# The last stage of an audio tower on one Trainium2 core: query and key parts stored so that each row of the stack is one run of memory

## What is computed

```python
def _L1_ffn_ref(x, hl_w, hl_b, wq, wk, wv, gate_w, ...):   # x: 32 x 375 x 64, nh=4 heads, ne=4 experts, d=16
    sx = jnp.einsum('bsh,ndh->bnsd', x, hl_w) + hl_b[None, :, None, :]
    q = jnp.einsum('bnsd,neod->bneso', sx, wq)
    k = jnp.einsum('bnsd,nod->bnso', sx, wk)
    v = jnp.einsum('bnsd,nod->bnso', sx, wv)
    scores = jnp.einsum('bnesd,bntd->bnest', q, k) * d ** 0.5 + causal
    att = jax.nn.softmax(scores, axis=-1)
    qkv = jnp.einsum('bnest,bntd->bnesd', att, v)
    ...
```

## Time and profile before

| what | us |
|---|---|
| median of 3 timed runs | 3450.6 (3449.06 to 3461.65) |
| the profiled execution | 3409.64 |
| its span, first to last instruction | 3407.9 |
| PE busy in it | 3063.6 (90%) |
| DVE, ACT, POOL busy | 2626.5, 1815.3, 1298.5 |

### The profile page before, as it was taken

The page is one execution under the profiler, slowest core; times in us unless marked ns, Lnnn a source line. Parts: engine busy times, 40 slices in busy tenths (PEclk is TensorE's granted clock), DMA queues, the critical chain, the costliest instruction groups (busy, mean ns, idle before and its releaser), DMA issues. The chain is left out here.

```text
span 3407.9 us, 81191 instructions
## 1 busy us (share of the span) xinstructions
PE 3063.6 (90%) x24976; PEld 2182.4 (64%) x24976; DVE 2626.5 (77%) x7757; ACT 1815.3 (53%) x4488; POOL 1298.5 (38%) x1365
## 2 busy tenths in 40 slices
PE   0799999999999799998999974999999999999995
PEld 0588888888788644445777752666666666666663
DVE  4788888888888578875888854688778778877883
ACT  0255555555555455554766631466556555555652
POOL 1443444434344144440000003355455445444532
PEclk9899999999999899996888865899999999989995
DMA  4100000000000000000000003335333444333420
GB/s 140 34 22 22 14 21 14 21 21 14 21 14 8 1 1 0 0 0 1 1 0 0 0 0 54 56 68 76 60 59 68 65 66 64 59 59 59 74 43 4
DMA packets 74286, 111.03 MB, mean 33 GB/s; under 512 B 20104, under 2 KB 65480, under 8 KB 73576
## 3 DMA queue, kind: packets, MB, share of 16 engines
q1 hardware_dynamic: 72936, 106.85, 16.8%
q10 hardware_dynamic: 1024, 0.39, 0.0%
HBM read 76.01 MB, written 30.82 MB: 31 GB/s over the span
## 5 line engine op out<-in xcount | busy, mean ns | idle before, releaser
L2698 DVE TENSOR_REDUCE qe_top<-psum 125x1 f32<-125x375 f32 (+2 forms) x896 | 500.2, 596 | 212.5 <-PE psum L2232 210.2
L2508 ACT ACTIVATE qe_E<-psum 125x375 f32<-125x375 f32 (+1 forms) x896 | 457.0, 531 | 262.9 <-PE psum L2232 244.9
L2232 PE MATMUL psum<-bconst 125*125 125x125 bf16 (+2 forms) x1792 | 482.2, 269 | 0.0
L624 PE MATMUL psum<-Q,K 96*125 96x125 f32 (+3 forms) x2304 | 405.0, 312 | 0.5 <-ACT E L835 0.4
L2243 PE MATMUL psum<-qe_K,qe_Q 96*125 96x375 bf16 (+2 forms) x1536 | 323.8, 294 | 58.0 <-DMA qe_K<-query_key_parts 28.8
L624 PEld LDWEIGHTS psum<-Q,K 96*125 96x125 f32 (+1 forms) x2304 | 334.9, 189 | 24.4 <-issue 1.2
L1174 POOL TENSOR_TENSOR Q<-rot 64x375 f32<-64x375 f32 (+1 forms) x256 | 305.8, 1214 | 73.4 <-DVE rot L975 61.4
L2255 PE MATMUL psum<-qe_Q,qe_K 97*125 97x375 bf16 (+2 forms) x1536 | 329.5, 294 | 2.2 <-ACT qe_E L2508 1.7
L835 ACT ACTIVATE E<-psum 125x500 f32<-125x500 f32 x384 | 226.2, 589 | 171.2 <-PE psum L644 168.0
L2243 PEld LDWEIGHTS psum<-qe_K,qe_Q 96*125 96x125 bf16 x1536 | 177.9, 144 | 162.1 <-DVE qe_top L2698 76.0
L2232 PEld LDWEIGHTS psum<-bconst 125*125 125x125 bf16 x1792 | 260.2, 145 | 9.7 <-issue 6.6
(11 more groups left out here) (354 smaller groups left out, 7213.2 us busy)
## 6 DMA issues: line engine op xcount, KB each, us to landing
qe_Q<-query_key_parts SPq DMA_DIRECT2D x192, 187.5 KB, 6.1
query_key_parts<-qe_parts SPq DMA_DIRECT2D x32, 843.8 KB, 3.6
s_row<-scores SPq DMA_DIRECT2D x32, 366.2 KB
qe_K<-query_key_parts SPq DMA_DIRECT2D x192, 46.9 KB, 6.6
x_tokens<-x SPq DMA_DIRECT2D x32, 187.5 KB
x_chunks<-x SPq DMA_DIRECT2D x4, 750.0 KB
E<-x SPq DMA_DIRECT2D x4, 750.0 KB
out<-qe_hout SPq DMA_DIRECT2D x32, 93.8 KB
```

The source lines that it names most:

```text
L624: nc.tensor.matmul(out[:, first * TP:(first + n) * TP].rearrange("p (o q) -> p o q", o=n), t.K[0:rows(h), par, h, jt * TP:(jt + 1) * TP], ...
L2232: return nc.tensor.matmul(out, B("ident_b")[0:TP, 0:TP], rhs, start=False, stop=True, skip_group_check=True)
L2508: nc.scalar.activation(E[:, e % 2, a:a + width], bank[0:TP, 4 + n % 2, 0:width], ACT.Exp).then_inc(e_done, 1)
L2698: nc.vector.tensor_reduce(dst, src, AX, ALU.max).then_inc(m_read, 1)
```

## The change

The rows of `parts` are put in another order, and DRAM is cut differently. Row 8d + 2n + e // 2 now holds a query, and row 8d + n a key (row 8d + 4 + n is zero), so that the eight query rows of one d follow each other, and the four key rows too. The order is that of the columns of `w_heads`, a constant made on the host; the values' columns stay as they were. In DRAM queries and keys are two regions, [part, row, 750] and [part, row, 375]. A row of `Q` is then one run of 8 x 1500 = 12000 bytes and a row of `K` one of 4 x 750 = 3000 bytes, while a row of `parts` goes to DRAM in six runs, three of 1500 and three of 750 bytes. The one store becomes two, each with a semaphore of its own; SP waits for both before the reads, ACT for both before it overwrites `parts`.

```diff
-    heads = z(D, 4, HE, 2, DH2)
+    queries, keys, values = z(D, 2, DH2, HE, 2), z(D, 1, DH2, 2, HE), z(D, 1, HE, 2, DH2)
...
-            heads[rows, e % 2, n, e // 2] = l["wq"][n, e].T
-        heads[rows, 2, n, 0] = l["wk"][n].T
-        heads[rows, 3, n, 0] = l["wv"][n].T
-    k.add("w_heads", heads.reshape(D, 4, 128))
+            queries[rows, e % 2, :, n, e // 2] = l["wq"][n, e].T
+        keys[rows, 0, :, 0, n] = l["wk"][n].T
+        values[rows, 0, n, 0] = l["wv"][n].T
+    k.add("w_heads", np.concatenate([v.reshape(D, -1, 128) for v in (queries, keys, values)], 1))
...
-            rows_of = qk_dram.rearrange("(a d) p i s -> p d a i s", d=DH2)
-            keys_of = qk_dram.rearrange("(h a d) p i s -> a p i d h s", a=2, d=DH2)
+            NQ = NP * 128 * 2 * S
+            queries = qk_dram[0:NQ].rearrange("(p r s) -> p r s", p=NP, r=128)
+            keys = qk_dram[NQ:].rearrange("(p r s) -> p r s", p=NP, r=128)
+            query_rows = queries.rearrange("p (d a) s -> p d (a s)", d=DH2)
+            key_rows = keys.rearrange("p (d h) s -> p d (h s)", d=DH2)
...
-                sp.dma_start(qk_dram, parts[:]).then_inc(parts_stored, 16)
+                sp.dma_start(queries.rearrange("p r s -> r p s"), parts[:, :, 0:2, :].rearrange("r p i s -> r p (i s)")
+                             ).then_inc(parts_stored, 16)
+                sp.dma_start(keys.rearrange("p r s -> r p s"), parts[:, :, 2, :]).then_inc(keys_stored, 16)
                 sp.wait_ge(parts_stored, (b + 1) * 16)
+                sp.wait_ge(keys_stored, (b + 1) * 16)
...
-                    sp.dma_start(Q[rows, slot].rearrange("d (a i) s -> d a i s", i=2), rows_of[qp, :, :, 0:2]
-                                 ).then_inc(stacked, 16)
-                    sp.dma_start(K[rows, slot], keys_of[0, kp, 2]).then_inc(stacked, 16)
+                    sp.dma_start(Q[rows, slot].rearrange("d q s -> d (q s)"), query_rows[qp]).then_inc(stacked, 16)
+                    sp.dma_start(K[rows, slot].rearrange("d h s -> d (h s)"), key_rows[kp, :, 0:HE * S]).then_inc(stacked, 16)
...
                 if i == 0:
                     wait(act, parts_stored, b * 16)
+                    wait(act, keys_stored, b * 16)
```

## The result

The changed kernel takes 3498.3 us (median of 6 runs, 3491.0 to 3509.6) where the kernel before takes 3448.2 on the same chip (6 runs, 3422.3 to 3461.7): a ratio of 1.017, interval 1.0135 to 1.0203. It is slower, outside the predicted range, and on the other side of the forecast. Its profiled execution took 3496.55 us.

What follows compares the result with a forecast made beforehand. PE, busy 90% of the span, was held by a closed loop through the stack's DMA latency. Taking 0.75 us off gave 4.6 (first rounds), 9.2 (ordinary), 4.7 and 2 (clock): 3450.6 - 20.5 = 3430 us, range 3406 to 3475.

Steps and rivals of the forecast that it cites:

- the term of the stores: Stack's stores: 40 more packets an engine and a second landing cost 0.35 us a round, bounded by 0.1 and 1.0.
- The reads: Stack's reads of Q and K: fewer, longer packets save 1.1 us a round, bounds 0 and some 5 us.
- The sum: Stack's latency: 0.35 - 1.1, so 0.75 us off a round, worth 20.5 us in all.
- The closed loop: Store to reads to PE and back: ordinary rounds lose what latency loses, and gain until PE is the limit.
- The clock: Two of 19 ordinary rounds fall to the low clock, 4.7 us each; half of the 9.4 us booked as gain.
- Rival (1): Reads keep their time, stores cost; none to four more low-clock rounds; 3459 to 3478 us, chance 0.22.
- ACT's added wait: ACT, before overwriting parts: costs nothing, since the store landed about 20 us earlier.
- the seven edges: PE's seven waits at the loop's edge, 23.3 us from 2300 to 3290 us: to stay as before.
- issues of SP: SP's read issues aren't shortened by fewer runs; twelve take 5 us against 12 us of data, costing nothing.
- the permuted weights: Matmuls on PE: the permuted weights leave every one as it was, at no cost.
- Rival (4): Long packets hold up instruction fetches on the shared DMA engines, feeding the loop; 3470 us or more, chance 0.03.
- Rival (2): Long packets let engines run ahead in the reads, latency falls by 2 us or more; 3416 us, chance 0.15.

Runs made afterwards that it cites:

- e5: e3 with the runs of the stores in DRAM at pitches of 1536 and 768 bytes instead of 1500 and 750; 3439.9 us, ratio 1.0028.
- e3: The kernel before with the change's two stores of 1500- and 750-byte runs, but the old row order and short reads; 3536.7 us, ratio 1.0261.
- e1: The kernel before with nine more already satisfied waits on SP between the store's landing and the first read; 3467.4 us, ratio 1.0054.
- e13: e5 with rows in DRAM at distances of 1600 and 832 bytes, multiples of 64; 3460.1 us, ratio 1.0127.
- e8: e4's early queries' store, but on the old rows, DRAM layout and short reads of the kernel before; 3402.9 us, ratio 0.9898.
- e4: The changed kernel with the queries' store issued once its parts are ready, ahead of the keys' store; 3378.3 us, ratio 0.980.
- e6: The kernel before with one store of nine 750-byte runs a row, DRAM laid out for long reads; 3527.1 us, ratio 1.0263.
- e12: The changed kernel with ACT waiting for the keys' store before its copy with i = 2 instead of i = 0; 3495.6 us, ratio 1.0206.
- e10: e5 with rows in DRAM at distances of 1504 and 800 bytes, multiples of 32; 3495.1 us, ratio 1.0231.
- e9: The changed kernel with rows of 375 numbers padded to 384 in tiles and DRAM, long reads kept; 3422.0 us, ratio 1.0015.
- e7: e4 with the six reads of Q issued before SP waits for the keys' store; 3369.2 us, ratio 0.9799.
- e11: e7 with rows of 375 numbers padded to 384 in tiles and DRAM; 3369.8 us, ratio 0.9853.
- e2: The kernel before with its store cut in two DMAs of 4500- and 2250-byte runs, same reads, both added waits; 3445.2 us, ratio 0.998.

## Why the prediction was wrong

**The failed step is the term of the stores.** It took the store's cost as 40 more packets an engine at 7 ns, 0.28, and 0.07 for a second landing: +0.35 us, bounded by 1.0. Measured from the first store's issue it was +1.52 us (5.12 - 3.60), above the upper bound. What the term did count, it priced well: e5's stores are cut the same way and only padded, and there store to first read is 3.98 us, 0.38 over before. What it put at nothing is the late landing of the unpadded runs, 1.14 us by e3 against e5 (5.12 - 3.98); the pause between the last packet and the landing is longer by 1.04 us than before (1.52 - 0.48). Nothing in the trace of before showed how long many short runs take to land after their last packet; its one store had 128 runs an item where the change has 768. The bound of 1.0 was a guess about the writes themselves ("short writes to DRAM cost twice") and not a row.

**The reads were right in kind.** Predicted -1.1 us, measured -0.74 (14.31 to 13.57), with 9,728 packets fewer (predicted 9,700). The term gave two thirds of what was asked of it. Its 7 ns fixed in a packet are doubtful: they came from a packet of a read and one of a store, and in the changed kernel's stores the means are 67 ns for 1500 bytes and 35 for 750, which leaves 3 (2 x 35 - 67). Its 142 ns for a packet of `K` stand in no row; over the reads of before the mean is 115.

The Trainium skill, "SBUF — State Buffer", section "Door 1: The DMA port swizzle", gives an asymptote of about 109 GB/s for 16 partitions, from which the prediction had estimated 13.2 us for the reads in either layout. The reads of the changed kernel (13.57 us) are nearer to it than those of before, but they did get shorter: before was further off the asymptote.

**The sum changed sign.** 1.52 - 0.74 = +0.78 us in place of -0.75. The closed loop then did what the prediction said of it, in the other direction; e1 shows it by itself. That the loop was read rightly is no luck; the direction was wrong by this one term.

**The clock was the second mistake.** The prediction saw that a round after a wait of 0.84 us had lost 4.7 us to the low clock, and booked half of two such falls. In all it turned 0.75 us of latency into 20.5 us, 27 us per microsecond. What the runs show, with the latency from one profiled execution and the time from the medians beside before on the same chip: the changed kernel +0.82 us and +50, e1 +0.34 and +17, e3 +1.48 and +86, e13 +0.51 and +33, e8 -0.48 and -31, e4 -1.17 and -72. That is 50 to 65 us per microsecond in both directions. Others lie outside it: e6 +1.15 and +93 (81), e12 +0.64 and +68 (107), e10 +0.46 and +76 (165), e5 +0.23 and +6 (25). So the price is well above 27 in nearly all of them, but it isn't one number. (For e4 and e8 the latency is counted from the last store, which ends what PE, ACT and POOL do for it.) The mean idleness at the first score matmul of the 19 ordinary rounds was 0.56 us before and 1.23 after; in these two profiles 2 of them had a fall of the clock, and 16. A change of latency moves rounds from the one kind to the other, 4.7 us each, and the whole chance of that should have been in the sum. The wait alone doesn't tell which round falls: in before the round from 2351.28 us stayed at full clock after 1.70 us. Rival (1) had the right sign and allowed up to four more falls; there were 14 in these rounds.

**ACT's added wait was called free, and it was, but the reason was wrong.** "The store landed about 20 us earlier" confused two items. In before ACT's copy starts 0.92 us after the landing of the store that it waits for (2642.38 against 2641.46), so a landing over 0.92 us later had to show there, and it did.

**Right**: the seven edges as before; issues of SP within the data's time; no effect of the permuted weights. Rival (4) isn't seen: e9 has the long packets and the time of before. Rival (2)'s pull of long packets, 2 us or more, didn't come; the 246 GB/s held against it was the mean of a window with 261 shorter packets beside the 57 long ones, and said little of long ones.

## What to carry to other kernels

A store's cost on a path is its landing, not its packets: before cutting a long run into short ones, look for the pause between the last packet and the waiter's release, and if the runs must be short, place them on boundaries (here 256 bytes, 768 and 1536 for 750 and 1500) or issue them before they are late. In a closed loop, first ask what can leave it: issuing the queries' store some 3 us earlier was worth 1% with the reads of before (e8) and 2% with the long ones (e4), more than any shaping of runs alone. And where PE's clock falls after some rounds' waits and not after others', price a microsecond of latency by the falls that it adds or takes away: here they made it worth more than twice what the waits themselves did, 50 us and more against at most 25.

The best kernel here is e7, 0.9799 (0.9769 to 0.9828) of the kernel before: the change's layout with the queries' store and reads ahead of the keys'. The runs don't tell e4 and e11 from it.

## What the runs showed of the hardware

**Many short writes off a boundary land late.** 768 runs an item of 1500 and 750 bytes, written at distances equal to their length: 1.52 us from last packet to landing (1.27 in e12, the same stores on another chip). The same at 1536 and 768 bytes: 0.40. Few long ones off a boundary don't: 128 runs of 6750 bytes 0.48, 256 of 4500 and 2250 (e2) 0.42. The Trainium skill, "Collectives: The Full Stack", section "Rules for kernel authors", asks for buffers of collectives aligned to 32 bytes, since that "Prevents HW read-modify-write". The rows agree in part: starts on 32 bytes bring most of it in the landing times (e10), but not all, and in the median time little. The Trainium skill, "DMA: Bandwidth & Descriptors", section "How a descriptor splits into AXI transactions", says of reads that a transaction must start at a 256-byte boundary; in its table 576 bytes that start off one take four transactions instead of three. No packet here took longer for it: 67 ns for 1500 bytes and 35 for 750 on the mean, in the changed kernel as in e5. If it matters for writes, it does so behind the packets.

**Whether it matters that neighbours share a block, is open.** The expectations of e5 and e9 put it so, and their kernels did what they said, but padding takes away both the sharing and the starts off a boundary. In e8 the queries' runs of 1500 bytes lie 2250 bytes apart, with the keys' places between them that this store doesn't write. It lands after 3.46 us, as late as e4's 3.51 without gaps. But its first packet starts 1.18 us after the issue instead of 0.90, and its pause is shorter, 0.53 us against 0.79, and 0.71 against 1.12 for the keys'. With e4's stores the queries' pause is 0.58 us in e7 and 0.36 padded in e11. So gaps may take part of the pause away; the runs don't settle how much. That a read-modify-write behind the packets is what takes the time, is argued only; no row shows it.

**Waits of a microsecond go with a lower clock, but not by their length alone.** In the changed kernel 16 of the 19 ordinary rounds ran at 1.2 GHz for 7 to 14 us from near their start. Their waits at the first matmul were 0.67 to 1.97 us; the rounds after waits of 0.65, 1.24 and 1.25 stayed at 2.4 GHz. In before the rounds after 0.84 and 0.73 us fell and those after 1.70, 1.27 and 0.97 didn't. Across all executions of the kernel before the mean granted clock goes from 0.921 at 3403.7 us to 0.903 at 3479.5, so by estimate 0.018 x 3440 = 62 of these 76 us are the clock's.
